# A state-space scan with a mixture of experts on one core: GpSimd makes two tiles of u by one instruction and adds dt's two parts

## The chip, the core and the metric

One core of a Trainium2 chip. The metric is the device time of one execution in microseconds (us). The text calls the engines TensorE (PE in rows), VectorE (DVE), ScalarE (ACT), GpSimd (POOL) and SyncE (SP, which only issues DMAs here; "SPq" in rows is its sequencer).

## What is computed

```python
xn = _layernorm(x)                      # x: 16 x 1024 x 256
dt = softplus(xn @ dt_w.T + dt_b)       # 256 features
A = -exp(log_A)                         # 256 x 32
b, c = xn @ B_w.T + B_b, xn @ C_w.T + C_b   # 32 states
h = exp(A * dt) * h + (dt * x) * b      # one step of time, 256 x 32 states
y = sum_n h * c + D_skip * x
out = x + y + moe(xn)                   # 8 experts, top 2, hidden 1024
```

softplus(v) is made as max(v, 0) + log(1 + exp(-|v|)): its first part and its logarithm are the "two parts" of dt.

## The kernel before, in words

After a preamble (layernorm, routing, the first dt values; it ends about 318 us into the execution) comes a loop over 128 **steps** on every engine. It is written as a loop over 8 experts whose body holds 16 steps written out, so every engine jumps back after each 16 steps.

The scan. A step covers 1024 time steps of one sequence and, of its 256 features and 32 states, 8 tiles `k` of 128 partitions (32 features x 4 states). Four steps (`ng` = 0 to 3) share one **half** of the features (`gh`), so a sequence is 8 steps and there are 32 halves in all. Of each tile:
- ScalarE makes the decay, `exp(a*dt)`, from tile `dt[k % 4]` into one of two PSUM buffers (`decay`, L798), two tiles ahead of the scan; `a_ready` counts them.
- GpSimd makes `u = dtx * b` into one of four SBUF buffers (L1027); `u_ready` counts them. A buffer comes free when the scan of four tiles before is done.
- VectorE scans (L1226) into `h`; `scan_done` counts. After tiles 0, 2, 4 and 6 it multiplies four tiles of `h` by `c` (`weigh`, L1215), and TensorE sums that over the states. The factor `c` is copied by ScalarE into PSUM bank 6 before each (`c_copy`, L868).

The prep. Each step also makes dt of 128 time steps for the next sequence: TensorE multiplies, ScalarE adds the bias into `zv` (L751), takes `|v|` and `exp` (L766, L768), and the logarithm into PSUM bank 6 (`log_part`, L772). At the end of the step VectorE forms `dt_n` from both by one instruction (`prep_dt`, L1131), and GpSimd multiplies it by x in the next step, after its tile 5 (`dtx_part`, L958). SyncE stores both in DRAM and the four tiles `dt` and the four tiles `dtx` are loaded from there when a new half begins: their loads are issued by SyncE during the **last step of a half** (`ng` = 3).

SyncE's order in that last step sets when these loads start. It works one list in order, each entry waiting for its own semaphores:

```python
next_b(0); next_dtx(0); store_dt; next_dtx(1); store_dtx; next_c(1)
next_dtx(2); next_dt(0); next_dtx(3); next_b(1)      # then w1, once in 16 steps
next_dt(1); next_dt(2); next_c(0); store_bc; next_dt(3)
```

(Written together here; in the code it is a list of calls with `if last:`.) `next_dtx(gp)` waits until u of tile 4 + gp of this step is made, `next_dt(gp)` until the decay of tile 4 + gp is.

The experts. Each step also pushes 256 slots through an expert: GpSimd gathers their rows by two indirect DMAs (L973) and scatters the result by two (L985); in two steps of eight it adds a block of y to the output by one more DMA (`add_y`, L990). TensorE works in program order: `moe_up(0), moe_up(1), quad(0), moe_up(2)`, the prep, `moe_up(3), quad(1)`, the transposes, `moe_down(0), quad(2), moe_down(1), quad(3)`; `quad(i)` sums the i-th weighing. ScalarE empties each product in between: `up_out` (L840) and `down_out` (L855), which stands behind the decay of the next step's tile 0 in ScalarE's own order; `c_copy(0)` stands behind the decay of the next step's tile 1, and `c_copy(2)` behind the emptying of the prep (`prep_out`), which waits for TensorE.

## Time and profile before

| what | value |
|---|---|
| median of 3 runs | 3790.76 us (3788.45 to 3792.91) |
| profiled execution, span | 3791.2 us |
| VectorE busy | 3645.0 us (96%) |
| GpSimd busy | 3268.7 us (86%) |
| TensorE busy | 3217.7 us (85%) |
| ScalarE busy | 2563.4 us (68%) |

The span of the profiled execution is taken as its time; it lies 0.4 us from the median. Busy shares are means over the preamble and the loop. "Idle before" in a row is idle time of the engine just before the instruction, and the arrow names what ended it.

### The profile page before, as it was taken

How to read it: one execution, taken by the hardware profiler on the slowest of the kernel's cores; microseconds unless marked ns; L12 is line 12 of the kernel's file. 1: busy time of each engine (PE TensorE's matmuls, PEld its weight loads, DVE VectorE, ACT ScalarE, POOL GpSimd, SP SyncE). 2: the span in 40 equal slices, each digit the busy share in tenths (PEclk: the TensorE clock that was granted, in tenths of full speed). 3: DMA queues.
4: the chain of work that ended last, by engine and by line, in shares of the span. 5: the costliest groups of instructions: out<-in, count | busy, mean ns of one | idle time of the engine just before them, and what ended most of it. 6: DMA issues, size and time to landing. Idle time of an engine off the chain costs nothing.

```text
span 3791.2 us, 64134 instructions
## 1 busy us (share of the span) xinstructions
PE 3217.7 (85%) x16548; PEld 2095.7 (55%) x16548; DVE 3645.0 (96%) x2281; ACT 2563.4 (68%) x4811; POOL 3268.7 (86%) x1722
## 2 busy tenths in 40 slices
PE   7776888888888888888888888888888888888887
PEld 4354555555555555555555555555555555555554
DVE  6787999999999999999999999999999999999998
ACT  3245677667776777767776777767776777677775
POOL 0017999999999999999999999999999999999996
PEclk9898999999999999999999999999999999999998
DMA  9974555555656556565656555465656555565666
GB/s 326 340 122 151 158 165 164 166 142 157 170 159 184 165 156 170 140 165 161 171 163 185 160 158 161 136 183 156 175 159 181 163 160 143 147 188 158 167 169 163
DMA packets 345249, 644.98 MB, mean 170 GB/s; under 512 B 49405, under 2 KB 221441, under 8 KB 344641
## 3 DMA queue, kind: packets, MB, share of 16 engines
q1 hardware_dynamic: 252018, 538.77, 44.1%
q0 software_dynamic: 67776, 85.24, 14.1%
q10 hardware_dynamic: 25104, 16.91, 2.0%
q8 instruction: 145, 2.38, 0.3%
q14 instruction: 206, 1.69, 0.1%
HBM read 515.55 MB, written 142.80 MB: 174 GB/s over the span
## 4 chain that ended last, share of the span: by engine, by line
DVE 36%; issue 28%; PE 9%; POOL 9%; ACT 8%; DMA 6%; DVEq 2%; SPq 1%; ACTq 0%; POOLq 0%
DVE hc L1215 18%; DVE h L1226 15%; POOL u L1027 5%; ACT bank L798 3%; DMA dt<-dt_rows 2%; PE bank L494 2%; PE bank L648 2%; PE bank L639 2%; POOL out_rows L985 2%; DMA dt<-x 2%; ACT xgt L802 1%; ACT za L766 1%; DVE dt_n L1131 1%; POOL xg L973 1%; ACT bank L868 1%
## 5 line engine op out<-in xcount | busy, mean ns | idle before, releaser
L1027 POOL TENSOR_TENSOR u<-dtx,b_sb 128x1024 f32<-128x1024 f32 x1024 | 2515.4, 2530 | 120.7 <-DVE h L1226 85.3
L1226 DVE TENSOR_TENSOR_SCAN h<-bank,u 128x1024 f32<-128x1024 f32 x1024 | 2301.8, 2279 | 17.4 <-POOL u L1027 11.5
L798 ACT ACTIVATE bank<-dt,a_neg 128x1024 f32<-128x1024 f32 x1026 | 1129.8, 1108 | 378.3 <-DVE h L1226 305.0
L639 PE MATMUL bank<-xgt,w_sb 128*128 128x256 f32 x4096 | 1027.9, 394 | 245.5 <-ACT ht L840 219.3
L1215 DVE TENSOR_TENSOR hc<-h,bank 128x2048 f32<-128x2048 f32 x514 | 1165.2, 2267 | 34.4 <-ACT bank L868 33.0
L639 PEld LDWEIGHTS bank<-xgt,w_sb 128*128 128x128 f32 x4096 | 745.6, 192 | 619.1 <-issue 536.2
L648 PE MATMUL bank<-w_sb,ht 128*128 128x256 f32 x4096 | 954.1, 387 | 26.0 <-ACT o_sb L855 24.6
L648 PEld LDWEIGHTS bank<-w_sb,ht 128*128 128x128 f32 x4096 | 774.4, 193 | 224.6 <-issue 125.3
L840 ACT ACTIVATE ht<-bank,b_sb 128x256 f32<-128x256 f32 x1024 | 423.6, 463 | 280.0 <-PE bank L639 279.9
L598 PE MATMUL bank<-hc,rsum 128*32 128x512 f32 x4112 | 549.3, 606 | 2.9 <-DVE hc L1215 2.9
L985 POOL DMA_INDIRECT out_rows<-o_sb,sidx x258 | 415.6, 1611 | 55.8 <-issue 34.5
L958 POOL TENSOR_TENSOR dtx_n<-dt_n,xnt 128x256 f32<-128x256 f32 x137 | 133.6, 975 | 272.3 <-DVE dt_n L1131 272.3
L973 POOL DMA_INDIRECT xg<-xn_rows,gidx x256 | 275.3, 1075 | 46.2 <-issue 44.2
L868 ACT ACTIVATE bank<-c_sb 128x512 f32<-128x512 f32 x512 | 303.1, 592 | 14.2 <-ACT bcv L756 2.8
L494 PE MATMUL bank<-ident,xg 128*128 128x128 f32 x516 | 87.2, 293 | 193.5 <-DVE hc L1215 178.6
L494 PEld LDWEIGHTS bank<-ident,xg 128*128 128x128 f32 x516 | 55.3, 143 | 310.0 <-DVE hc L1215 292.9
L598 PEld LDWEIGHTS bank<-hc,rsum 128*32 128x32 f32 x4112 | 80.9, 108 | 187.8 <-issue 184.1
L650 PE MATMUL bank<-b_row,ones 1*128 x512 | 177.7, 426 | 0.0
L855 ACT ACTIVATE o_sb<-bank,gate 128x256 f32<-128x256 f32 x256 | 119.4, 467 | 76.5 <-PE bank L650 70.3
L541 PE MATMUL bank<-xnt,dtw 128*128 128x128 f32 (+1 forms) x1104 | 151.1, 280 | 16.8 <-DVE hc L1215 14.2
L541 PEld LDWEIGHTS bank<-xnt,dtw 128*128 128x128 f32 x1104 | 137.2, 191 | 40.9 <-issue 35.5
L751 ACT ACTIVATE zv<-bank,dtb 128x128 f32<-128x128 f32 x276 | 86.5, 364 | 99.5 <-PE bank L548 98.1
(114 smaller groups left out, 1819.0 us busy)
## 6 DMA issues: line engine op xcount, KB each, us to landing
b_sb<-bc_rows SPq DMA_DIRECT2D x258, 512.0 KB
c_sb<-bc_rows SPq DMA_DIRECT2D x258, 512.0 KB, 4.0
dt<-dt_rows SPq DMA_DIRECT2D x132, 512.0 KB, 8.0
dtx<-dtx_rows SPq DMA_DIRECT2D x132, 512.0 KB, 5.2
w_sb<-w SPq DMA_DIRECT2D x18, 1024.0 KB
dt_rows<-dt_n SPq DMA_DIRECT2D x137, 128.0 KB
dtx_rows<-dtx_n SPq DMA_DIRECT2D x137, 128.0 KB
out_rows<-y_sb POOLq DMA_DIRECT2D x34, 512.0 KB
```

The lines of the kernel that those rows point to most:

```text
L541: mm = pe.matmul(z_ps[:, g * Q:(g + 1) * Q], dtw[:, k, g * P:(g + 1) * P], src, start=(k == 0), stop=(k == KD - 1))
L598: mm = pe.matmul(y_ps[c * RD:(c + 1) * RD, th, :], rsum[:], hc[:, GPP * th + c, :], start=False, stop=True, skip_group_check=True, tile_po ...
L639: mm = pe.matmul(m_ps[:, c, :], w1_sb[:, kk, ch * P:(ch + 1) * P], xgt[:, kk, :], start=(kk == 0), stop=(kk == KD - 1))
L648: pe.matmul(m_ps[:, j, :], ht[:, c, j * P:(j + 1) * P], w2_sb[:, c, :], start=(c == 0), stop=False)
L798: act.activation(a_ps[k % 2], dt[:, k % GPP, :], ACT.Exp, scale=a_neg[:, col:col + 1]).then_inc(a_ready, 1)
L840: ins = act.activation(ht[:, ch, :], m_ps[:, c, :], ACT.Relu, bias=b1_sb[:, bass.ds(e * HC + ch, 1)])
L868: act.activation(c_ps, c_sb[:, j, th * HALF:(th + 1) * HALF], ACT.Copy).then_inc(c_ready, 1)
L973: pool.indirect_dma_start(xg[:, buf, j, :], None, xn_d, rows, bounds_check=T - 1, oob_is_err=False).then_inc(xg_in, 16)
L985: pool.indirect_dma_start(outf, rows, o_sb[:, buf, j, :], None, bounds_check=T - 1, oob_is_err=False, compute_op=ALU.add).then_inc(o_scatt ...
L1027: pool.tensor_tensor(u[:, k % UB, :], dtx[:, gp, :], b_sb[:, j, :], ALU.mult).then_inc(u_ready, 1)
L1215: dve.tensor_tensor(hc[:, GPP * th:GPP * (th + 1), :], h[:, GPP * j:GPP * (j + 1), th * HALF:(th + 1) * HALF], c_ps.unsqueeze(1).to_broadc ...
L1226: dve.tensor_tensor_scan(h[:, k, :], a_ps[k % 2], u[:, k % UB, :], 0.0, ALU.mult, ALU.add).then_inc(scan_done, 1)
```

## The change

GpSimd makes tiles 2m and 2m+1 of u by one instruction of 2048 columns, with `b` broadcast over both, so a step has 4 of them where it had 8; `u_ready` counts pairs. A pair waits for the scans that free both its buffers, and at the start of a half for both tiles of `dtx`. Everything that waited for one tile of u waits for its pair. The instruction that forms `dt_n` leaves VectorE's loop; GpSimd does it in the next step, after its second pair, and `dtx_part` follows it there directly. [...] In the preamble VectorE still forms `dt_n`, but for the last one.

```diff
-        zv = sb("zv", [P, KD, Q])
+        zv = sb("zv", [P, 2, KD, Q])
+        zl = sb("zl", [P, 2, KD, Q])
...
+        NPR = NG // 2
...
                     def next_dtx(gp):
-                        sp.wait_ge(u_ready, st * NG + 4 + gp + 2)
+                        sp.wait_ge(u_ready, st * NPR + 2 + gp // 2 + 2)
...
                     def next_b(j):
-                        sp.wait_ge(u_ready, st * NG + 4 * j + 3 + 2)
+                        sp.wait_ge(u_ready, st * NPR + 2 * j + 1 + 2)
...
-            def softplus(p):
-                act.activation(za[:], zv[:], ACT.Abs).then_inc(za_done, 1)
+            def softplus(p, buf):
+                act.activation(za[:], zv[:, buf], ACT.Abs).then_inc(za_done, 1)
                 act.wait_ge(za_done, p + 1)
                 act.activation(ze[:], za[:], ACT.Exp, scale=-1.0).then_inc(ze_done, 1)
+                act.activation(zv[:, buf], zv[:, buf], ACT.Relu)
...
-                act.activation(zl_ps, ze[:], ACT.Ln, bias=1.0).then_inc(l_done, 1)
+                act.activation(zl[:, buf], ze[:], ACT.Ln, bias=1.0).then_inc(l_done, 1)
...
                         if i == 0:
                             act.wait_ge(c_in[1], 16 * (st + 2))
-                            act.wait_ge(dt_done, p + 2)
+                            act.wait_ge(hc_done, 4 * st + 5)
...
+            def dt_sum(p, buf):
+                pool.wait_ge(l_done, p + 1)
+                pool.wait_ge(dt_st, 16 * p + 1)
+                pool.wait_ge(prep_done, p + 1)
+                settle(pool)
+                pool.tensor_tensor(dt_n[:], zv[:, buf], zl[:, buf], ALU.add).then_inc(dt_done, 1)
...
-                    for k in range(NG):
-                        j, gp = k // GPP, k % GPP
+                    for m in range(NPR):
+                        j, gp = m // 2, 2 * (m % 2)
                         if gp == 0:
                             pool.wait_ge(b_in[j], 16 * (st + 1))
-                        if ng == 0 and k < GPP:
-                            pool.wait_ge(dtx_in[gp], 16 * (hf + 1))
-                        pool.wait_ge(scan_done, st * NG + k - UB + 1 + SCAN0)
-                        pool.tensor_tensor(u[:, k % UB, :], dtx[:, gp, :], b_sb[:, j, :], ALU.mult).then_inc(u_ready, 1)
+                        if ng == 0 and m < 2:
+                            for g in (gp, gp + 1):
+                                pool.wait_ge(dtx_in[g], 16 * (hf + 1))
+                        pool.wait_ge(scan_done, st * NG + 2 * m + 1 - UB + 1 + SCAN0)
+                        pool.tensor_tensor(u[:, gp:gp + 2, :], dtx[:, gp:gp + 2, :],
+                                           b_sb[:, j, :].unsqueeze(1).to_broadcast([P, 2, S]), ALU.mult).then_inc(u_ready, 1)
...
-                        if k == 5:
+                        if m == 1:
+                            dt_sum(NG + 1 + st, (s + 1) % 2)
                             dtx_part(NG + 1 + st, (b + 1 + (s + 1) // NG) % 2, (s + 1) % NG)
-                        if k in (4, 6):
-                            scatter(st, (s + 1) % 2, k // 2 - 2, 2 * b + ng if adds else None)
+                        if m >= 2:
+                            scatter(st, (s + 1) % 2, m - 2, 2 * b + ng if adds else None)
...
                 for k in range(NG):
-                    dve.wait_ge(u_ready, st * NG + k + 2)
+                    if k % 2 == 0:
+                        dve.wait_ge(u_ready, st * NPR + k // 2 + 2)
...
-                prep_dt(NG + 2 + st)
```

How GpSimd's order moves. In the middle of a step, before, from tile 4 on: u, a scatter, u of tile 5, the product `dtx_n`, and then (not shown) u of tile 6, a scatter, u of tile 7.

```order
L1027 TENSOR_TENSOR u<-dtx,b_sb 128x1024 [waits scan_done]
L980 ISA [waits sidx_done]
L985 DMA out_rows<-o_sb,sidx 16384x256 [waits evac_done]
L1026 REGISTER_ALU
L1027 TENSOR_TENSOR u<-dtx,b_sb 128x1024 [waits scan_done]
L955 REGISTER_ALU
L956 ISA [waits dt_done]
L958 TENSOR_TENSOR dtx_n<-dt_n,xnt 128x256 [waits dtx_st]
L1026 REGISTER_ALU
```

Now, from the second pair (tiles 2 and 3) on:

```order
L1039 TENSOR_TENSOR u<-dtx,b_sb 128x2048 [waits scan_done]
L984 DMA xg<-xn_rows,gidx 128x258
L959 ISA [waits l_done]
L962 TENSOR_TENSOR dt_n<-zv,zl 128x256 [waits dt_st,prep_done]
L966 REGISTER_ALU
L969 TENSOR_TENSOR dtx_n<-dt_n,xnt 128x256 [waits dt_done,dtx_st]
L1038 REGISTER_ALU [waits b_in1]
L1039 TENSOR_TENSOR u<-dtx,b_sb 128x2048 [waits scan_done]
L991 ISA [waits sidx_done]
L996 DMA out_rows<-o_sb,sidx 16384x256 [waits evac_done]
```

The sum and the product stand together between the second and the third pair, and the scatters behind the third and the fourth.

How SyncE's order stands in the last step of a half. It reads the same before and after (here: after), but its waits for `u_ready` are now for pairs: the first `dtx` row below needs the fourth pair, tiles 6 and 7, where it needed tile 6.

```order
L339 DMA dtx<-dtx_rows 128x1x1024 [waits u_ready,dtx_st]
L417 ISA
L339 DMA dt<-dt_rows 128x1x1024 [waits a_ready,dt_st]
L339 DMA dtx<-dtx_rows 128x1x1024 [waits u_ready,dtx_st]
L328 ISA [waits u_ready,b_st]
L328 ISA
L328 DMA b_sb<-bc_rows 128x1x1024
L417 REGISTER_ALU
L339 DMA dt<-dt_rows 128x1x1024 [waits a_ready,dt_st]
```

The rows are `next_dtx(2)`, `next_dt(0)`, `next_dtx(3)`, `next_b(1)`, `next_dt(1)`; nothing in them changed places.

## Rows read from the trace of the kernel before

**Rows 1.** The page's first line
```profile
span 3791.2 us, 64134 instructions
```

**Rows 2.** Groups of instructions: busy us, mean ns | idle before, its releasers
```profile
L1027 POOL TENSOR_TENSOR u<-dtx,b_sb 128x1024 f32<-128x1024 f32 x1024 | 2515.4, 2530 | 120.7 <-DVE h L1226 85.3 <-issue 21.7
L1226 DVE TENSOR_TENSOR_SCAN h<-bank,u 128x1024 f32<-128x1024 f32 x1024 | 2301.8, 2279 | 17.4 <-POOL u L1027 11.5 <-ACT bank L798 5.7
L798 ACT ACTIVATE bank<-dt,a_neg 128x1024 f32<-128x1024 f32 x1026 | 1129.8, 1108 | 378.3 <-DVE h L1226 305.0 <-DMA dt<-dt_rows 48.8 <-issue 17.3
```

**Rows 3.** Timeline of VectorE, one undisturbed step: start us, us, what, idle before
```profile
1940.97 0.40 DVE L1131 SCALAR_TENSOR_TENSOR dt_n<-zv,bank 128x256 f32<-128x256 f32 x1
1941.28 2.29 DVE L1226 TENSOR_TENSOR_SCAN h<-bank,u 128x1024 f32<-128x1024 f32 x1
...
1967.85 2.29 DVE L1226 TENSOR_TENSOR_SCAN h<-bank,u 128x1024 f32<-128x1024 f32 x1
```

**Rows 4.** Timeline of GpSimd around the start of a step with add_y
```profile
550.85 0.73 POOL L958 TENSOR_TENSOR dtx_n<-dt_n,xnt 128x256 f32<-128x256 f32 x1
551.54 2.37 POOL L1027 TENSOR_TENSOR u<-dtx,b_sb 128x1024 f32<-128x1024 f32 x1
554.06 1.60 POOL L985 DMA_INDIRECT out_rows<-o_sb,sidx  x1 [0.16 <-issue]
555.13 5.25 POOL L1027 TENSOR_TENSOR u<-dtx,b_sb 128x1024 f32<-128x1024 f32 x2
559.75 1.98 POOL L990 DMA_DIRECT2D out_rows<-y_sb  x1
562.03 1.11 POOL L973 DMA_INDIRECT xg<-xn_rows,gidx  x1 [0.30 <-issue]
...
566.81 7.01 POOL L1027 TENSOR_TENSOR u<-dtx,b_sb 128x1024 f32<-128x1024 f32 x3
```

**Rows 5.** Timelines at an undisturbed half's end: SyncE, ScalarE, VectorE
```profile
1927.80 0.54 SPq L338 DMA_DIRECT2D dt<-dt_rows  x1
...
1936.71 1.12 ACT L798 ACTIVATE bank<-dt,a_neg 128x1024 f32<-128x1024 f32 x1 [0.65 <-DVE h L1226]
...
1956.60 2.27 DVE L1215 TENSOR_TENSOR hc<-h,bank 128x2048 f32<-128x2048 f32 x1
```

**Rows 6.** Timelines at the loop's first half's end: SyncE
```profile
420.90 0.54 SPq L338 DMA_DIRECT2D dtx<-dtx_rows  x1
421.63 0.54 SPq L338 DMA_DIRECT2D dt<-dt_rows  x1
```

**Rows 7.** The same stretch, ScalarE
```profile
429.06 1.12 ACT L798 ACTIVATE bank<-dt,a_neg 128x1024 f32<-128x1024 f32 x1 [4.10 <-DMA dt<-dt_rows]
...
433.86 1.12 ACT L798 ACTIVATE bank<-dt,a_neg 128x1024 f32<-128x1024 f32 x1 [3.02 <-DMA dt<-dt_rows]
```

**Rows 8.** The same stretch, VectorE; it started this step at the first row
```profile
403.40 2.28 DVE L1226 TENSOR_TENSOR_SCAN h<-bank,u 128x1024 f32<-128x1024 f32 x1
...
431.62 2.29 DVE L1226 TENSOR_TENSOR_SCAN h<-bank,u 128x1024 f32<-128x1024 f32 x1
435.62 2.29 DVE L1215 TENSOR_TENSOR hc<-h,bank 128x2048 f32<-128x2048 f32 x1 [1.71 <-ACT bank L868]
...
450.49 2.29 DVE L1215 TENSOR_TENSOR hc<-h,bank 128x2048 f32<-128x2048 f32 x1 [1.65 <-ACT bank L868]
```

**Rows 9.** Timeline of TensorE, moe_down(1) in the same stretch and in another step
```profile
430.71 6.06 PE L648 MATMUL bank<-w_sb,ht 128*128 128x256 f32 x16 [3.65 <-ACT o_sb L855]
...
2019.42 3.72 PE L648 MATMUL bank<-w_sb,ht 128*128 128x256 f32 x16
```

**Rows 10.** Windows, columns: us, busy (x instructions) by engine, PEclk, DMA share, GB/s
```profile
431.00:434.00 3.00, 3.00 (x8) 2.37 (x8) 2.71 (x2) 0.14 (x1) 2.97 (x2) 0.50 1.03 400
```

**Rows 11.** Timeline of ScalarE across a jump back of the expert loop
```profile
2049.46 1.12 ACT L798 ACTIVATE bank<-dt,a_neg 128x1024 f32<-128x1024 f32 x1 [3.69 <-DMA dt<-dt_rows]
...
2055.52 1.12 ACT L798 ACTIVATE bank<-dt,a_neg 128x1024 f32<-128x1024 f32 x1 [3.94 <-issue]
```

More of the change, by code:

```diff
@@ L551, in prep @@
             def prep(p, par, q):
-                pe.wait_ge(dt_done, p + 1)
+                pe.wait_ge(bcv_done, p)
                 prep_z(par, q)
@@ L614, in _ @@
             pe.wait_ge(map_ready, 1)
-            pe.wait_ge(dt_done, NG + 3)
+            pe.wait_ge(bcv_done, NG + 2)
             pe.wait_ge(xg_in, 16 * SJ)
@@ L778, in low_part @@
                                scale=tokval[:, 0:1]).then_inc(low_ready, 1)
-            with act.Fori(0, NG) as q:
-                for o in range(OHQ):
-                    low_part(q * OHQ + o, o % 2)
-                    if o == 0:
-                        evac_prep(q)
-                        act.wait_ge(v_done, q + 1)
-                    if o == 1:
-                        softplus(q)
-                    if o == 2:
-                        log_part(q)
+            with act.Fori(0, NG // 2) as qq:
+                for i in range(2):
+                    q = qq * 2 + i
+                    for o in range(OHQ):
+                        low_part(q * OHQ + o, o % 2)
+                        if o == 0:
+                            evac_prep(q, i)
+                            act.wait_ge(v_done, q + 1)
+                        if o == 1:
+                            softplus(q, i)
+                        if o == 2:
+                            log_part(q, i)
             for p in (NG, NG + 1):
-                evac_prep(p)
+                evac_prep(p, p % 2)
                 act.wait_ge(v_done, p + 1)
-                softplus(p)
-                log_part(p)
+                softplus(p, p % 2)
+                log_part(p, p % 2)
             def decay(k, col):
@@ L925, in _ @@
                             act.wait_ge(v_done, p + 1)
-                            softplus(p)
+                            softplus(p, s % 2)
                             c_copy(3)
@@ L1019, in _ @@
                     adds = gh == 0 and ng in (1, 2)
-                    for k in range(NG):
-                        j, gp = k // GPP, k % GPP
+                    for m in range(NPR):
+                        j, gp = m // 2, 2 * (m % 2)
                         if gp == 0:
                             pool.wait_ge(b_in[j], 16 * (st + 1))
-                        if ng == 0 and k < GPP:
-                            pool.wait_ge(dtx_in[gp], 16 * (hf + 1))
-                        pool.wait_ge(scan_done, st * NG + k - UB + 1 + SCAN0)
-                        pool.tensor_tensor(u[:, k % UB, :], dtx[:, gp, :], b_sb[:, j, :], ALU.mult).then_inc(u_ready, 1)
-                        if k == 0 and adds:
+                        if ng == 0 and m < 2:
[4 more added lines that the diff above has]
+                                           b_sb[:, j, :].unsqueeze(1).to_broadcast([P, 2, S]), ALU.mult).then_inc(u_ready, 1)
+                        if m == 0 and adds:
                             pool.wait_ge(y_evac, 2 * hf + ng + 1)
@@ L1032, in _ @@
                             add_y((hf + 2 * B - 2 + ng - 1) % (2 * B), ng - 1)
-                        if k < SJ:
-                            gather(st + 1, (s + 1) % 2, k)
-                        if k == 5:
+                        if m < SJ:
+                            gather(st + 1, (s + 1) % 2, m)
+                        if m == 1:
+                            dt_sum(NG + 1 + st, (s + 1) % 2)
                             dtx_part(NG + 1 + st, (b + 1 + (s + 1) // NG) % 2, (s + 1) % NG)
-                        if k in (4, 6):
-                            scatter(st, (s + 1) % 2, k // 2 - 2, 2 * b + ng if adds else None)
+                        if m >= 2:
+                            scatter(st, (s + 1) % 2, m - 2, 2 * b + ng if adds else None)
             for j in range(SJ):
@@ L1130, in prep_dt @@
                 dve.wait_ge(prep_done, p + 1)
-                dve.scalar_tensor_tensor(out=dt_n[:], in0=zv[:], scalar=0.0, in1=zl_ps,
+                dve.scalar_tensor_tensor(out=dt_n[:], in0=zv[:, buf], scalar=0.0, in1=zl[:, buf],
                                          op0=ALU.max, op1=ALU.add).then_inc(dt_done, 1)
@@ L1180, in pairs @@
                 return t[:, bass.ds(g * OHB, OHB)].rearrange("p (i r) -> p i r", r=2).unsqueeze(2).to_broadcast([P, OHP, n, 2])
-            with dve.Fori(0, NG) as q:
-                for o in range(OHQ):
-                    g, buf = q * OHQ + o, o % 2
-                    dve.wait_ge(oh_used, g + 1)
-                    settle(dve)
-                    dve.tensor_tensor(oh_p[:, buf], wide(iota_pair, P), pairs(prt_h, g, P), ALU.is_equal).then_inc(ohp_done, 1)
-                    dve.tensor_tensor(oh_c[:, buf], wide(iota_pair, E * LPE), pairs(col_h, g, E * LPE), ALU.is_equal)
-                    dve.wait_ge(ohp_done, g + 1)
-                    dve.tensor_tensor(oh_high[:, buf], oh_p[:, buf], pairs(num_h, g, P), ALU.mult).then_inc(oh_ready, 1)
-                prep_dt(q)
-            prep_dt(NG)
-            prep_dt(NG + 1)
+            with dve.Fori(0, NG // 2) as qq:
+                for i in range(2):
+                    q = qq * 2 + i
+                    for o in range(OHQ):
+                        g, buf = q * OHQ + o, o % 2
+                        dve.wait_ge(oh_used, g + 1)
+                        settle(dve)
+                        dve.tensor_tensor(oh_p[:, buf], wide(iota_pair, P), pairs(prt_h, g, P), ALU.is_equal).then_inc(ohp_done, 1)
+                        dve.tensor_tensor(oh_c[:, buf], wide(iota_pair, E * LPE), pairs(col_h, g, E * LPE), ALU.is_equal)
+                        dve.wait_ge(ohp_done, g + 1)
+                        dve.tensor_tensor(oh_high[:, buf], oh_p[:, buf], pairs(num_h, g, P), ALU.mult).then_inc(oh_ready, 1)
+                    prep_dt(q, i)
+            prep_dt(NG, 0)
             dve.wait_ge(oh_used, 2 * NT // OHB + 2)
```

20 lines of the change are left out of this document (9 added, 11 removed).

## Prediction

> **What bounds the kernel now.** I read the page, then the groups, then timelines. The profiled execution spans 3791.2 us [rows 1], 0.4 us over the median of 3790.76, so the sum is made against 3791. The groups put the scans first on VectorE, with 17.4 us of idle time before 1024 of them; u on GpSimd, with 120.7 us, is the runner-up [rows 2]. The timeline of VectorE gives the pace: a step from its first scan to the next step's is 1967.85 - 1941.28 = 26.57 us, without a gap [rows 3]. Nearly all of the 128 steps have this length, so VectorE bounds the loop. What is off that pace is at the ends of halves, and there the transfers of the new half decide; that is where I put most of the working.
>
> **The removed instruction.** From the start of dt_n to the start of the scan behind it is 1941.28 - 1940.97 = 0.31 us [rows 3]; its own 0.40 overlaps its neighbour. A step of VectorE becomes 26.26 us, a pair of tiles with its weighing 6.565. That gives -0.31 x 128 = **-40 us**. Nothing hides it: VectorE is the bound.
>
> **GpSimd's new step.** A tile of u costs 7.01 / 3 = 2.34 us and dtx_n, 256 columns, 0.69 (550.85 to 551.54) [rows 4]. Between them lie 768 columns: 2.15 ns each and 0.14 fixed, so a pair of 2048 is 4.54. The bounds are 4.4 (columns alone) and 5.06 (twice the group's mean of 2.53 [rows 2], which counts overlapped time). A gather takes 1.11 and some 0.17 of issue, a scatter 1.07 + 0.16 and makes the next u later by 5.25 - 4.68 = 0.57, so 1.8; add_y adds 562.03 - 560.38 - 0.16 = 1.5 in two steps of eight [rows 4]. The sum of dt is like dtx_n, 0.69; the product now waits for it to be complete, for which I add 0.15 (estimate, by the gaps of 0.16 there). Together 4 x 4.54 + 2 x 1.28 + 2 x 1.8 + 2 x 0.69 + 0.15 = 25.85, where it was 8 x 2.34 + 2.56 + 3.6 + 0.69 = 25.57. GpSimd stays 0.4 us under VectorE's 26.26. For the add alone, 0.69 on GpSimd replaces 0.31 on VectorE. The Trainium skill (GPSIMD Engine Reference, Performance versus the Vector engine) would leave it where it was: its rule is that ordinary elementwise work stays on VectorE, since GpSimd is about half as fast. By the rule the move loses 0.38 us a step, by the trace it gains 0.31, since the engine that gets slower is not the bound.
>
> But the coupling is coarser. Pair m can start only when VectorE has begun pair m-1, and must be there 6.565 later: it may start late by 6.565 - 4.54 - 0.1 = 1.9 us. The lateness changes by 4.54 + what follows - 6.565: -0.7 after pair 0 (a gather), +0.8 after pair 1 (gather, sum, product), -0.2 after pairs 2 and 3. In an ordinary step it peaks at 0.9 and pair 3 starts 0.6 late: hidden. With add_y in two steps in a row it reaches 1.9 and VectorE waits about 1 us in eight steps: 16 x 1 = **+16 us** (bounds 0 and 25, by pairs of 4.4 and 4.7). The first pair of all is made while VectorE waits: **+2 us**. Relu on ScalarE stands between the exp and `c_copy(3)`. A decay of 1024 columns takes 1.12 [rows 7], so 256 take at most 0.5 (estimate). In an undisturbed step no weighing waits for a copy [rows 3], the scans of tiles 5 and 6 cover it, so I take nothing; without that cover it would be up to 0.5 x 128 = 64. The preamble keeps its instructions: 0.
>
> **The ends of halves.** SyncE issues the load of dt tile 0 behind that of dtx tile 2, which waited for u of tile 6. Before, it went out at 1927.80, 13.1 us after its step began (1941.28 - 26.57 = 1914.71), and the decay that needs it started at 1936.71, having waited for the scan alone [rows 3, 5]: in time. Now tile 6 comes with tile 7, whose buffer is free after the scan of tile 3: 2 x 6.565 = 13.1 us into the step. Add 0.6 of lateness and 4.54: 18.3; the loads go out one by one, 0.73 apart (420.90 to 421.63) [rows 6]: dt tile 0 at about 19.1, **6 us later** than before, the others behind it.
>
> The trace of before has one half's end just like that. In the loop's first steps GpSimd was still behind, and dt tile 0 was issued at 421.63, 18.2 us after the step's start at 403.40 [rows 6, 8]. The decay waited 4.10 us for it until 429.06, and the next decay 3.02 for tile 1 [rows 7]. The step after began at 431.62, where 403.40 + 26.57 = 429.97 was due; its first weighing waited 1.71 more [rows 8], as `c_copy(0)` stands behind the second decay. Then comes what costs most: `down_out(0)` stands behind the first decay, so TensorE waited 3.65 us for it, and took 6.06 us for sixteen products that take 3.72 elsewhere [rows 9], at a granted clock of 0.50, the lower level (1.2 GHz) [rows 10]. From there TensorE and ScalarE work without slack to `c_copy(2)`, and VectorE waited 1.65 for it until 450.49 [rows 8]. That is 450.49 - 403.40 = 47.1 us after the step's start; undisturbed it is 1956.60 - 1914.71 = 41.9 [rows 5]. This end cost **5.2 us**.
>
> There are 31 ends of halves inside the loop. In the new kernel each has this delay, 0.9 us worse (19.1 against 18.2), against a due time 0.31 earlier: 5.2 + 0.9 + 0.3 = 6.3 us, rounded down for what the two estimates are worth. At 23 of them nothing was lost before: 23 x 6.3 = **+145 us**. The first is the one above: +1. At 7 the expert loop jumps back and an expert's weights are loaded too; there the decays already waited 3.69 us for dt tile 1 and 3.94 for the jump [rows 11]. The dt tiles come some 5 us later there as well, but part of it falls beside the waits that exist; I take 4, **+28 us** (bounds 1 and 7). For the 23 the bounds are 3 (the two waits of VectorE at the step's start, 1.65 and 1.71, and TensorE's part absorbed) and 7.5 (a further 1.2 if the pairs are late by the 1.9 that they may be).
>
> **The sum:** 3791 - 40 + 16 + 2 + 145 + 1 + 28 = 3943; I say **3940 us**, 3.9% slower.
>
> **Rivals.**
> - *The loads still come in time (faster).* The load of dt tile 0 has from 19.1 to the end of scan 6, 22.0 us after the step's start (1936.71 - 1914.71), to land: 2.9 us. In favour: 7.4 us in rows 6 and 7 were measured among other transfers. Against: it would have to be less than half that. It decides at a landing time of about 3 us. Then -40 + 16 + 2 = -22: **3769 us**.
> - *Late, but cheap.* The two decays are late and TensorE's chain takes it up, as its wait is shorter or the clock stays up: 3 us at 23 ends, 1 at 7. 3791 - 40 + 18 + 69 + 7 = **3845 us**. Rows 8 speak against it: the third wait is as long as each of the others.
> - *GpSimd becomes the bound in every step.* A pair costs 5.06 and not 4.54: a step of GpSimd is 25.85 + 2.1 + 0.4 (add_y, mean) = 28.3, 1.8 over the old 26.57. 128 x 1.8 = 225, in which the ends' waits lie for the most part: about **4020 us**. For it: 0.4 us is thin. Against: one tile alone takes 2.37, and the mean of 2.53 holds what overlaps the tail of a scatter, 5.25 for two against 4.68 [rows 4].
> - *The change doesn't do what it says:* if the removed 0.31 came back as a wait (for the copy of c, which waited for dt_n and now for the weighing), only the -40 would go: 3983 us. Against: the copy has the 2.28 us of the next scan [rows 2, 3], and behind a decay of 1.12 [rows 7] needs some 0.6 of them (estimate: half the columns).
>
> **How the numbers follow.** Forecast 0.66; cheap delay 0.17; loads in time 0.06; GpSimd bound 0.09; the gain not there 0.02. A measurement of this kernel tells 0.2% (about 8 us) from no change. Only the second rival's lower edge comes near no change: its cost would have to be 1 us an end. I give 0.05 to that and 0.06 to faster, which leaves 0.89 for slower. The forecast's own bounds: 3791 - 40 + 69 + 7 + 2 = 3829 at the low end, 3791 - 40 + 25 + 2 + 173 + 2 + 49 = 4002 at the high one. They take in the cheap delay and the gain not there, and leave out the faster case and part of the third rival. Range **3825 to 4000**.
>
> **What would show it.** VectorE's undisturbed step at 26.26 us. The group of u at 4.5 us, x512, and little idle time before scans for u. At the ends of halves: SyncE issues dt tile 0 some 19 us into the step, ScalarE's decay waits 4 to 5 us for it, the decays' idle time put down to the load of dt grows from 48.8 us [rows 2] to 200 or more, and VectorE's weighings wait for the copy of c by over 100 us in all. TensorE's granted clock falls at each end. The prediction is wrong if the ends of halves keep the pace of their neighbours (then the landing time is what I misjudged), if ordinary steps are longer than 26.3 (then a pair costs more than 4.54), or if the load of dt is not behind that of dtx tile 2.

## The result and the profile after

The changed kernel takes **3952.11 us** (median of 4 runs, 3948.33 to 3960.42) against 3790.54 for the kernel before: a ratio of **1.0425, interval 1.0407 to 1.0443**. The forecast was 3940. The profiled execution spans 3946.5 us, 155.3 more than before [rows 1], and the working below is against that.

The first lines of the page of the changed kernel:

```profile
span 3946.5 us, 62062 instructions
...
PE 3281.4 (83%) x16548; PEld 2144.6 (54%) x16548; DVE 3617.5 (92%) x2152; ACT 2579.6 (65%) x4949; POOL 3291.3 (83%) x1338
```

VectorE is busy 27.5 us less than before (3645.0), and the span is 155 longer: the loss is idle time. The groups of instructions (busy us, mean ns | idle before, its releasers), which answer to [rows 2], say in front of what:

```profile
L1039 POOL TENSOR_TENSOR u<-dtx,b_sb 128x2048 f32<-128x2048 f32 x512 | 2411.0, 4709 | 241.1 <-DVE h L1242 194.4 <-DMA dtx<-dtx_rows 45.0 <-issue 0.3
L1242 DVE TENSOR_TENSOR_SCAN h<-bank,u 128x1024 f32<-128x1024 f32 x1024 | 2293.0, 2273 | 59.7 <-ACT bank L802 36.9 <-POOL u L1039 22.3
L1230 DVE TENSOR_TENSOR hc<-h,bank 128x2048 f32<-128x2048 f32 x514 | 1164.5, 2266 | 181.0 <-ACT bank L872 169.9 <-PE bank L599 10.0 <-ACT bank L943 0.7
L802 ACT ACTIVATE bank<-dt,a_neg 128x1024 f32<-128x1024 f32 x1026 | 1128.2, 1107 | 516.6 <-DVE h L1242 265.4 <-DMA dt<-dt_rows 230.2 <-issue 20.5
L649 PE MATMUL bank<-w_sb,ht 128*128 128x256 f32 x4096 | 1031.4, 409 | 147.7 <-ACT o_sb L859 147.7
```

GpSimd is not the bound: scans waited 22.3 us in all for u. The decays waited 230.2 us for the load of dt, where it was 48.8. The weighings waited 169.9 us for the copy of c, and TensorE's `moe_down` 147.7 us for an eviction of `o_sb`. The same two groups of the kernel before have 33.0 and 24.6 there:

```profile
L1215 DVE TENSOR_TENSOR hc<-h,bank 128x2048 f32<-128x2048 f32 x514 | 1165.2, 2267 | 34.4 <-ACT bank L868 33.0 <-ACT bank L940 0.7
...
L648 PE MATMUL bank<-w_sb,ht 128*128 128x256 f32 x4096 | 954.1, 387 | 26.0 <-ACT o_sb L855 24.6 <-issue 1.4
```

The timeline of VectorE over a quiet step and the end of a half (start us, us, what, idle before):

```profile
1840.64 2.26 DVE L1230 TENSOR_TENSOR hc<-h,bank 128x2048 f32<-128x2048 f32 x1
...
1866.88 2.26 DVE L1230 TENSOR_TENSOR hc<-h,bank 128x2048 f32<-128x2048 f32 x1
...
1888.74 2.28 DVE L1242 TENSOR_TENSOR_SCAN h<-bank,u 128x1024 f32<-128x1024 f32 x1
1892.14 2.29 DVE L1242 TENSOR_TENSOR_SCAN h<-bank,u 128x1024 f32<-128x1024 f32 x1 [1.12 <-ACT bank L802]
1896.47 2.29 DVE L1230 TENSOR_TENSOR hc<-h,bank 128x2048 f32<-128x2048 f32 x1 [2.03 <-ACT bank L872]
...
1911.62 2.29 DVE L1230 TENSOR_TENSOR hc<-h,bank 128x2048 f32<-128x2048 f32 x1 [1.92 <-ACT bank L872]
...
1938.47 2.29 DVE L1230 TENSOR_TENSOR hc<-h,bank 128x2048 f32<-128x2048 f32 x1 [0.47 <-ACT bank L872]
```

From the first weighing of one step to that of the next is 1866.88 - 1840.64 = **26.24 us**; before it was 26.57 [rows 3]. The last step of the half starts at 1864.68 (its first weighing less the 2.20 of a scan), and at its end the three waits that the prediction took from [rows 8] stand in a row: for the decay of tile 0, for `c_copy(0)`, for `c_copy(2)`. A fourth, 0.47, comes a step later, in front of the third weighing again; the prediction didn't have it.

SyncE's queue in that last step:

```profile
1883.36 0.55 SPq L339 DMA_DIRECT2D dtx<-dtx_rows  x1
1884.18 0.54 SPq L339 DMA_DIRECT2D dt<-dt_rows  x1
```

dt tile 0 goes out 1884.18 - 1864.68 = 19.5 us into the step; 13.1 before [rows 5]. (On the mean of the 23 ordinary ends it is 19.9 against 13.0.) ScalarE at the same end:

```profile
1890.91 1.12 ACT L802 ACTIVATE bank<-dt,a_neg 128x1024 f32<-128x1024 f32 x1 [4.57 <-DMA dt<-dt_rows]
1891.96 0.46 ACT L859 ACTIVATE o_sb<-bank,gate 128x256 f32<-128x256 f32 x1
...
1894.71 1.12 ACT L802 ACTIVATE bank<-dt,a_neg 128x1024 f32<-128x1024 f32 x1 [1.99 <-DMA dt<-dt_rows]
1895.77 0.58 ACT L872 ACTIVATE bank<-c_sb 128x512 f32<-128x512 f32 x1
...
1898.42 0.48 ACT L859 ACTIVATE o_sb<-bank,gate 128x256 f32<-128x256 f32 x1 [2.07 <-PE bank L651]
```

The two decays wait for dt tiles 0 and 1, and behind each stands what others wait for: `down_out(0)` behind the first, `c_copy(0)` behind the second. TensorE's side of it:

```profile
1892.56 5.11 PE L649 MATMUL bank<-w_sb,ht 128*128 128x256 f32 x16 [4.51 <-ACT o_sb L859]
```

and the window over these 16 products (us, busy by engine, PEclk, DMA share, GB/s):

```profile
1892.50:1897.50 5.00, 4.94 (x16) 4.00 (x16) 2.97 (x2) 1.86 (x3) 4.84 (x2) 0.71 0.94 377
```

After a wait of 4.51 us the granted clock is 0.71 on the mean of the five microseconds, between the two levels (0.50 is the 1.2 GHz one), and the products take 5.11 us where 3.72 is usual [rows 9, 10]. DMA is at 0.94: the load is not alone.

GpSimd in a quiet step, for the price of a pair and of the new sum:

```profile
2061.91 4.54 POOL L1039 TENSOR_TENSOR u<-dtx,b_sb 128x2048 f32<-128x2048 f32 x1 [0.78 <-DVE h L1242]
2066.61 1.06 POOL L984 DMA_INDIRECT xg<-xn_rows,gidx  x1 [0.16 <-issue]
2067.69 0.73 POOL L962 TENSOR_TENSOR dt_n<-zv,zl 128x256 f32<-128x256 f32 x1
2068.63 0.73 POOL L969 TENSOR_TENSOR dtx_n<-dt_n,xnt 128x256 f32<-128x256 f32 x1 [0.20 <-POOL dt_n L962]
2069.31 4.55 POOL L1039 TENSOR_TENSOR u<-dtx,b_sb 128x2048 f32<-128x2048 f32 x1
```

It still waits 0.78 us for VectorE: there is lead, as the 25.85 against 26.26 said.

For the whole loop I took the length of each of the 128 steps from the timeline of VectorE, before and after. "Excess" is what is over the quiet pace of the same kernel; an "ordinary" end is one inside the body of 16 steps, without the first.

| part | before, us | after, us | in the sum |
|---|---|---|---|
| quiet step | 26.57 | 26.24 | -0.33 x 128 = -42 |
| excess of an ordinary half's end (23) | 0.0 | 6.1 | +140 |
| excess of an end at the loop's jump (7) | 4.96 | 9.3 | +30 |
| the first end | 5.2 | 6.6 | +1 |
| the third step of each sequence, its second with `add_y` (16) | 0.04 | 0.7 | +11 |
| the step behind an end (31) | 0.1 | 0.6 | +17 |
| first scan of the loop, start | 321.97 | 316.65 | -5 |
| behind the loop | | | +4 |

These make 156 of the 155.3.

### The profile page after: what moved, and what is told of

Its sections match the earlier page's. It is cut to its first block, busy times and chain, and to the rows that moved or that the text cites. A ratio compares the mean times of both kernels' runs of the same rounds, so it can differ in the third digit from the quotient of the medians.

```text
span 3946.5 us, 62062 instructions
## 1 busy us (share of the span) xinstructions
PE 3281.4 (83%) x16548; PEld 2144.6 (54%) x16548; DVE 3617.5 (92%) x2152; ACT 2579.6 (65%) x4949; POOL 3291.3 (83%) x1338
## 4 chain that ended last, share of the span: by engine, by line
issue 43%; POOL 23%; PE 13%; DMA 12%; ACT 4%; DVE 2%; SPq 1%; POOLq 1%; ACTq 0%; DVEq 0%
POOL u L1039 13%; PE bank L649 6%; DMA out_rows<-o_sb,sidx 5%; POOL xg L984 4%; POOL out_rows L996 4%; PE bank L640 3%; DMA dtx<-dtx_rows 2%; DMA dt<-x 2%; POOL dt_n L962 2%; PE bank L599 1%; DMA dtx_rows<-dtx_n 1%; DMA dt<-dt_rows 1%; ACT ht L844 1%; ACT bank L802 1%; PE bank L651 1%
## 5 line engine op out<-in xcount | busy, mean ns | idle before, releaser
L1039 POOL TENSOR_TENSOR u<-dtx,b_sb 128x2048 f32<-128x2048 f32 x512 | 2411.0, 4709 | 241.1 <-DVE h L1242 194.4
L1242 DVE TENSOR_TENSOR_SCAN h<-bank,u 128x1024 f32<-128x1024 f32 x1024 | 2293.0, 2273 | 59.7 <-ACT bank L802 36.9
L1230 DVE TENSOR_TENSOR hc<-h,bank 128x2048 f32<-128x2048 f32 x514 | 1164.5, 2266 | 181.0 <-ACT bank L872 169.9
L640 PE MATMUL bank<-xgt,w_sb 128*128 128x256 f32 x4096 | 1020.1, 392 | 242.9 <-ACT ht L844 221.4
L649 PE MATMUL bank<-w_sb,ht 128*128 128x256 f32 x4096 | 1031.4, 409 | 147.7 <-ACT o_sb L859 147.7
L640 PEld LDWEIGHTS bank<-xgt,w_sb 128*128 128x128 f32 x4096 | 740.2, 190 | 613.9 <-issue 532.9
L649 PEld LDWEIGHTS bank<-w_sb,ht 128*128 128x128 f32 x4096 | 828.0, 207 | 369.4 <-issue 246.8
L969 POOL TENSOR_TENSOR dtx_n<-dt_n,xnt 128x256 f32<-128x256 f32 x137 | 125.1, 913 | 287.7 <-DVE dt_n L1145 241.3
```

The lines of the kernel that those rows point to most:

```text
L640: mm = pe.matmul(m_ps[:, c, :], w1_sb[:, kk, ch * P:(ch + 1) * P], xgt[:, kk, :], start=(kk == 0), stop=(kk == KD - 1))
L649: pe.matmul(m_ps[:, j, :], ht[:, c, j * P:(j + 1) * P], w2_sb[:, c, :], start=(c == 0), stop=False)
L1039: pool.tensor_tensor(u[:, gp:gp + 2, :], dtx[:, gp:gp + 2, :], b_sb[:, j, :].unsqueeze(1).to_broadcast([P, 2, S]), ALU.mult).then_inc(u_re ...
L1230: dve.tensor_tensor(hc[:, GPP * th:GPP * (th + 1), :], h[:, GPP * j:GPP * (j + 1), th * HALF:(th + 1) * HALF], c_ps.unsqueeze(1).to_broadc ...
L1242: dve.tensor_tensor_scan(h[:, k, :], a_ps[k % 2], u[:, k % UB, :], 0.0, ALU.mult, ALU.add).then_inc(scan_done, 1)
```

## The experiments

The theory: at each half's end the load of dt tile 0 is issued 6 us later, because it stands behind a load that waits for a pair; what that delays costs 6 us at 23 ends and 4 more than before at 7. Rivals: the pairs themselves or the sum on GpSimd cost the time in ordinary steps; Relu on ScalarE does; the ends are dear because of the amount that is moved there, in whatever order; or it is not the load as such but the order of ScalarE behind it.

**The loads of dt ahead of those of dtx tiles 2 and 3** (`e1_dt_first`), the rest as changed:

```diff
                     if last:
-                        next_dtx(2)
                         next_dt(0)
+                        next_dt(1)
+                        next_dt(2)
+                        next_dtx(2)
                         next_dtx(3)
...
-                    if last:
-                        next_dt(1)
-                        next_dt(2)
```

> The changed kernel, but SyncE issues the loads of dt tiles 0, 1 and 2 ahead of those of dtx tiles 2 and 3. Theory A (the late load of dt behind the pair of u makes the ends of halves dear): dt tile 0 goes out 3 us earlier, about 16.6 us into the step, the two waits at the step's start shrink to under 1.5 us together, but dtx tiles 2 and 3 land later and the second pair costs about 1.3; an end costs 1.5 to 2.5 where it cost 6.1: about 3835 us, between 3800 and 3870. Theory B (the ends are dear because of the amount moved there at once, whatever the order): stays at 3950 within 15 us.

Measured: 3850.81 us, ratio 1.0157 (1.0140 to 1.0174). 101 of the 162 us are gone by reordering five issues. An ordinary end costs 2.5 us in place of 6.1. But dtx tiles 2 and 3 are late now, and the groups show the new wait in front of the scans:

```profile
L1241 DVE TENSOR_TENSOR_SCAN h<-bank,u 128x1024 f32<-128x1024 f32 x1024 | 2297.3, 2276 | 119.4 <-POOL u L1038 85.7 <-ACT bank L801 32.2
```

It was 22.3 us for u in the changed kernel.

**The same delay put into the kernel before** (`e3_before_late`): neither pairs nor the moved sum, only a wait of SyncE.

```diff
                         next_dtx(2)
+                        sp.wait_ge(scan_done, st * NG + 5 + 1 + SCAN0)
+                        settle(sp)
                         next_dt(0)
```

> The kernel before, with one thing more: in the last step of a half SyncE waits for the scan of tile 5 before it loads dt tile 0, so that this load goes out about 20 us into the step where it went out at 13.1. Nothing of GpSimd, VectorE or ScalarE is changed. Theory A: an end costs about 6 us as in the changed kernel, 23 x 6 + 7 x 4 + 1: about 3960 us, between 3930 and 3985. Theory B' (the pairs of u or the sum on GpSimd cost it): stays at 3791 within 15 us.

Measured: 3909.09 us, ratio 1.0308 (1.0291 to 1.0326): a late issue alone costs 118 us, so the mechanism is the right one, but the size is 51 us under what I expected, and 21 under the lower bound. SyncE and then ScalarE, in a last step that starts at 1849.30:

```profile
1869.32 0.53 SPq L338 DMA_DIRECT2D dt<-dt_rows  x1
...
1873.90 1.12 ACT L800 ACTIVATE bank<-dt,a_neg 128x1024 f32<-128x1024 f32 x1 [3.19 <-DMA dt<-dt_rows]
...
1879.03 1.12 ACT L800 ACTIVATE bank<-dt,a_neg 128x1024 f32<-128x1024 f32 x1 [3.34 <-DMA dt<-dt_rows]
```

The issue is at 20.0, as late as in the changed kernel, but the decay starts at 1873.90 - 1849.30 = 24.6 and not at 26.2. Here dtx tile 2 went out long before (7.7 us); in the changed kernel it goes out 0.82 us ahead of dt tile 0. The trace has the landings too: from issue to landing dt tile 0 takes 4.1 us here and 6.3 in the changed kernel (medians of the 23 ordinary ends). An end costs 3.3 us, and the third wait, for `c_copy(2)`, is 0.4 us on the mean against 1.8. The load's place in the row is a second part of the delay, next to the time of its issue.

**Each half of the change alone.** `e4_single_u` is the changed kernel with u tile by tile, `e5_pairs_only` the kernel before with the pairs (and VectorE's sum as it was).

```diff
-                        pool.wait_ge(scan_done, st * NG + 2 * m + 1 - UB + 1 + SCAN0)
-                        pool.tensor_tensor(u[:, gp:gp + 2, :], dtx[:, gp:gp + 2, :],
-                                           b_sb[:, j, :].unsqueeze(1).to_broadcast([P, 2, S]), ALU.mult).then_inc(u_ready, 1)
+                        pool.wait_ge(scan_done, st * NG + k - UB + 1 + SCAN0)
+                        pool.tensor_tensor(u[:, k % UB, :], dtx[:, gp, :], b_sb[:, j, :], ALU.mult).then_inc(u_ready, 1)
```

> The changed kernel with u made tile by tile again (8 instructions a step, buffers freed one by one); the sum of dt stays on GpSimd, after tile 5. GpSimd's step is 8 x 2.34 + 2.56 + 3.6 + 1.38 + 0.2 = 26.4 us against VectorE's 26.24, so it loses its lead slowly, above all in the two steps with add_y. Theory A: the load of dt tile 0 goes out at about 14 us in one half of a sequence and at 17 in the other, so every second end costs about 2: 3791 - 42 + 32 - 5 = 3776, between 3750 and 3805. If the sum on GpSimd (and not the pairs) were what makes the changed kernel slow: over 3900.

Measured: 3828.53 us, ratio 1.0104 (1.0087 to 1.0121), 53 over the expectation and outside its range. Quiet steps are 26.24 as planned. But GpSimd now does all the old work and the sum besides. In the halves with `add_y`, which use up its lead, dt tile 0 goes out 15.4 us into the last step in the first sequence of an expert and 17.7 in the second, and an end costs 2.0 and 3.7 us; in the other halves inside an expert it goes out at 14.6 and an end costs 0.6. The sum on GpSimd is not free by itself: its 0.7 us come out of the lead that the loads live on.

> The kernel before with u made in pairs, and nothing else: dt_n stays on VectorE. Theory A: steps of 26.57, ends of halves as dear as in the changed kernel: 3791 + 23 x 6 + 7 x 4 + 1 = 3958, between 3935 and 3980. If the sum on GpSimd were the cause: within 15 us of 3791.

Measured: 3938.35 us, ratio 1.0396 (1.0377 to 1.0416), 148 over the kernel before, of 162 in all. Quiet steps are 26.57, an end costs 4.9, and the decay of dt tile 0 starts 25.5 us into the step. So the pairs make most of the loss, and not by their price: the group of u has a mean of 4709 ns for two tiles in the changed kernel, less than twice the 2530 of [rows 2].

**dt tile 0 loaded ahead of dtx tile 0, dt tile 1 ahead of dtx tile 2** (`e6_dt_before_dtx`):

```diff
                     if last:
+                        next_dt(0)
                         next_dtx(0)
...
                     if last:
+                        next_dt(1)
                         next_dtx(2)
-                        next_dt(0)
                         next_dtx(3)
...
                     if last:
-                        next_dt(1)
                         next_dt(2)
```

> The changed kernel, with SyncE loading dt tile 0 ahead of dtx tile 0 in the last step of a half (about 11 us into the step, where its decay is made), tile 1 ahead of dtx tile 2, tile 2 behind b. Theory A: dt tiles 0 and 1 land before they are wanted, the waits of the decays for them nearly vanish, and with them TensorE's wait and fall of the clock; dtx tiles 2 and 3 land a little late. An end costs 0 to 2 us where it cost 6.1, the waits of 0.6 in the step after an end go as well: 3952 - 23 x 5 - 7 x 3 - 12 = 3804, between 3780 and 3835. Theory B (the amount moved): above 3850, as the first reordering left it.

Measured: **3781.62 us** (10 runs), ratio **0.9975 (0.9966 to 0.9985)**: all of the loss is gone and the kernel is 8.5 us faster than the one before. SyncE and ScalarE at the end whose last step starts at 1795.8:

```profile
1806.14 0.56 SPq L339 DMA_DIRECT2D dt<-dt_rows  x1
...
1817.81 1.12 ACT L802 ACTIVATE bank<-dt,a_neg 128x1024 f32<-128x1024 f32 x1 [0.34 <-DVE h L1242]
...
1822.19 1.12 ACT L802 ACTIVATE bank<-dt,a_neg 128x1024 f32<-128x1024 f32 x1 [2.56 <-DVE h L1242]
```

Issued at 10.3; the decays wait for the scans again, as in [rows 5]. The groups of the weighings and of `moe_down`:

```profile
L1230 DVE TENSOR_TENSOR hc<-h,bank 128x2048 f32<-128x2048 f32 x514 | 1162.3, 2261 | 28.2 <-ACT bank L872 27.0 <-ACT bank L943 0.7
...
L649 PE MATMUL bank<-w_sb,ht 128*128 128x256 f32 x4096 | 955.2, 387 | 21.2 <-ACT o_sb L859 21.2
```

An ordinary end costs 0.4 us. The pairs, the sum on GpSimd, Relu and the amount moved are the changed kernel's; only SyncE's order differs. No run puts this order into the kernel before, so how the 8.5 us are shared between the change and the new order is not shown.

**The order of ScalarE, with the loads late as they are.** `e7_down_first` takes `down_out(0)` ahead of the decay of tile 0 in last steps; `e8_down_and_copy` also `c_copy(0)` ahead of that of tile 1; `e10_act_three` also `down_out(1)`. The last of them:

```diff
+                        if tng == 0 and k == 6:
+                            down_out(0)
+                        if tng == 0 and k == 7:
+                            c_copy(0)
+                            down_out(1)
                         if tng == 0 and tk < GPP:
                             act.wait_ge(dt_in[tk], 16 * (2 * b + ts // HPB + 1))
...
                         if k == 6:
-                            down_out(0)
+                            if tng != 0:
+                                down_out(0)
...
                         if k == 7:
-                            c_copy(0)
-                            down_out(1)
+                            if tng != 0:
+                                c_copy(0)
+                            if tng != 0:
+                                down_out(1)
```

> The changed kernel, its loads untouched; in the last step of a half ScalarE empties the product of moe_down(0) before the decay of the next half's tile 0, not behind it. Theory A says that the third wait of an end (1.9 us before weighing 2, and 0.5 in the step after) comes only through TensorE, which waits for that emptying and is at the low clock afterwards. Then this wait goes and the first two (1.2 before the scan, 2.2 before the first weighing) stay: an end costs 3.7: 3952 - 23 x 2.4 - 7 x 1.5 - 15 = 3871, between 3850 and 3895. If the third wait had its cause in the late loads of dt tiles 2 and 3 or of c instead, nothing changes (3952 within 10).

Measured: 3946.93 us, ratio 1.0408 (1.0385 to 1.0430): 5 us gained where 81 were expected, and even those 5 are within the spread of the runs (3936.35 to 3954.19, the changed kernel's 3948.33 to 3960.42). TensorE at such an end, and a window over its last row (columns as above):

```profile
1892.04 3.72 PE L649 MATMUL bank<-w_sb,ht 128*128 128x256 f32 x16
...
1901.42 3.75 PE L640 MATMUL bank<-xgt,w_sb 128*128 128x256 f32 x8 [4.04 <-ACT o_sb L859]
...
1901.40:1905.20 3.80, 3.75 (x8) 2.51 (x8) 3.80 (x2) 0.98 (x1) 2.42 (x3) 0.50 0.62 194
```

`moe_down(1)` takes its usual 3.72 without a wait. The wait has gone one place on, to `moe_up(0)`, which needs the bank that `down_out(1)` empties, and that one stands behind the second decay. Its eight products take 3.75 us where they take 1.99 undisturbed, at a granted clock of 0.50. In the groups 147.7 us of wait at L649 have become 13.7, and 130.5 new ones stand at L640:

```profile
L640 PE MATMUL bank<-xgt,w_sb 128*128 128x256 f32 x4096 | 1098.2, 415 | 355.6 <-ACT ht L844 219.6 <-ACT o_sb L859 130.5 <-ACT xgt L806 4.4
```

So this run moved TensorE's wait and its low clock; it didn't take them away.

> As the run with the emptying first, and the copy of c for the first weighing also stands ahead of the decay of tile 1. Theory A: the wait of 2.2 before the first weighing goes too; what is left is the scan that waits 1.2 for the decay of tile 0, and at most 0.5 before the scan of tile 1: an end costs 1.2 to 2, 23 x 4.4 + 7 x 4 + 15 less than the changed kernel: 3808, between 3785 and 3835, with the loads as late as ever.

Measured: 3928.46 us, ratio 1.0368 (1.0346 to 1.0391), also a miss, by 120 us. The weighings' wait for the copy halves (169.9 to 84.9), and the scans' wait for decays grows from 36.9 to 112.1:

```profile
L1248 DVE TENSOR_TENSOR_SCAN h<-bank,u 128x1024 f32<-128x1024 f32 x1024 | 2293.8, 2274 | 135.5 <-ACT bank L802 112.1 <-POOL u L1045 23.2
L1236 DVE TENSOR_TENSOR hc<-h,bank 128x2048 f32<-128x2048 f32 x514 | 1163.6, 2264 | 89.3 <-ACT bank L872 84.9 <-ACT bank L949 4.3
```

The decays themselves start when they did (26.4 and 30.6 us into the last step at an ordinary end, 26.3 and 30.3 in the changed kernel). VectorE, no longer held at the weighing, comes to the scans earlier and waits there. TensorE still waits 120.8 us at L640 for `down_out(1)`.

> The changed kernel with its loads as late as ever; in the last step of a half ScalarE empties both products of moe_down and makes the copy of c ahead of the decays for which it waits. The runs before left TensorE waiting one place further on (4.0 us behind the second emptying, which stood behind the decay of tile 1). If that chain is the cause of the third wait, it goes now: an end costs the 1.2 before the scan, up to 0.5 before the next and little else: 3952 - 23 x 4 - 7 x 3 - 15 = 3824, between 3795 and 3850. If the third wait comes from the late tiles 2 and 3 of dt or from c, it stays and the time is near 3928.

Measured: 3876.74 us, ratio 1.0222 (1.0206 to 1.0238), 53 over the expectation and outside its range. ScalarE at the end whose last step starts at 1832.9:

```profile
1855.35 0.48 ACT L859 ACTIVATE o_sb<-bank,gate 128x256 f32<-128x256 f32 x1 [0.84 <-PE bank L651]
1858.71 1.12 ACT L802 ACTIVATE bank<-dt,a_neg 128x1024 f32<-128x1024 f32 x1 [2.88 <-DMA dt<-dt_rows]
...
1860.07 0.58 ACT L872 ACTIVATE bank<-c_sb 128x512 f32<-128x512 f32 x1
1860.62 0.47 ACT L859 ACTIVATE o_sb<-bank,gate 128x256 f32<-128x256 f32 x1
1862.56 1.12 ACT L802 ACTIVATE bank<-dt,a_neg 128x1024 f32<-128x1024 f32 x1 [1.46 <-DMA dt<-dt_rows]
```

The decay of tile 0 starts at 25.8 (26.4 on the mean), as late as ever, and an ordinary end costs 2.5 us instead of 6.1. So some 3.6 of the 6.1 is what three small instructions of ScalarE make of the late loads by standing behind the decays, TensorE's wait and low clock included: TensorE's waits for an eviction of `o_sb` are down to 13.4 us at L649 and 5.5 at L640. Of the 2.5 left, 1.1 is VectorE's wait for the late decay of tile 0 and 0.9 still its wait for `c_copy(2)`. The third instruction, `down_out(1)`, brings 52 of the 75 us, with the other two already moved; it alone was not tried. What lies over the expectation is in the 2.5 left at each ordinary end (23 x 2.5 = 57 us in all) and at the loop's jumps, where a step became longer rather than shorter (31.6 us for 30.9, 10 us over 14 steps).

**The two cures together**, to see what is left: `e9_all_pairs` (e6 and e8), `e11_pairs_best` (e6 and e10), `e12_single_best` (the same with single tiles of u).

> Both: the loads of dt early and ScalarE's two instructions ahead of its decays, with pairs of u. An end costs 0 to 1 us; left are the two steps with add_y (0.7 in eight steps: 12 us) and the jumps of the loop (about 4 each, as before the change). 3791 - 42 - 5 + 12 + 10 = 3766, between 3750 and 3790, so faster than the kernel before.

> Pairs of u, early loads of dt, and ScalarE's three instructions ahead of its decays. The ends already cost next to nothing with the early loads; what is left are add_y's two steps (1.5 us in eight) and the jumps of the loop (4.5 each), where the second emptying could save 1 to 2: 3775, between 3765 and 3785.

> The same with u tile by tile. GpSimd's step is 26.4 us and 27.9 with add_y, 214.4 in eight steps against VectorE's 209.9, so GpSimd bounds the kernel on the mean, though it never stops VectorE for its pairs: 16 x 214.4 + 340 = 3770, between 3760 and 3785. If it is well above the version with pairs, the pairs are worth having once the loads are early.

Measured: 3784.08 (0.9984, 0.9974 to 0.9994), 3784.77 (0.9975, 0.9963 to 0.9987), 3786.06 (0.9983, 0.9975 to 0.9992). The first two came out at or near the upper edge of what was expected, the third 1 us above its range. With the loads in time ScalarE's order has nothing left to mend, and pairs or single tiles make no difference that these runs can tell. e6 is as fast as any of them with the fewest edits.

**Relu done twice** (`e13_relu_twice`), with a wait between. (In the changed kernel ScalarE applies Relu to `zv` in place, one more instruction of 256 columns a step; it takes 0.40 us.)

```diff
+                act.activation(zv[:, buf], zv[:, buf], ACT.Relu).then_inc(relu_done, 1)
+                act.wait_ge(relu_done, p + 1)
                 act.activation(zv[:, buf], zv[:, buf], ACT.Relu)
```

> The changed kernel with the Relu done twice (with a wait between, so some 0.45 us more on ScalarE in each step, ahead of the copy of c for weighing 3). If the Relu is covered, as the prediction says, 3952 within 8 us; if it lies on the path, up to 0.45 x 128 = 58 more.

Measured: 3955.25 us, ratio 1.0429 (1.0414 to 1.0444), against 1.0425: no difference. A Relu here is covered.

The ends, on the mean of the 23 ordinary ones. The decay of tile 0 is counted from the last step's start; the third wait is VectorE's for `c_copy(2)`; the low clock is the time at a granted clock of 0.50 in the stretch from 22 to 50 us after the last step's start.

| kernel | decay of tile 0, us | third wait, us | low clock, us | an end costs, us |
|---|---|---|---|---|
| before | 22.0 | 0 | 0 | 0.0 |
| e6 | 22.2 | 0.1 | 0 | 0.4 |
| e3 | 24.3 | 0.4 | 3.0 | 3.3 |
| e5 | 25.5 | 1.9 | 5.3 | 4.9 |
| changed | 26.3 | 1.8 | 5.6 | 6.1 |
| e7 (same loads, ScalarE's order changed) | 26.4 | 1.3 | 7.1 | 5.7 |
| e8 (the same) | 26.4 | 1.6 | 5.9 | 4.9 |
| e10 (the same) | 26.4 | 0.9 | 2.5 | 2.5 |

## Why the prediction was right, point by point

- **The removed instruction**, -0.31 a step by the gap between starts: measured -0.33, -42 us for -40. Taking the gap and not the duration of 0.40 was right.
- **A pair at 4.54**, the sum like `dtx_n`, 0.15 for the dependence: 4.54, 0.73 and 0.20. The group's mean of 4709 ns is again above one that runs alone; whoever had taken it would have seen GpSimd as the bound. The third rival falls.
- **`add_y` +16:** about +11. The rule of the Trainium skill (GPSIMD Engine Reference, Performance versus the Vector engine) that elementwise work stays on VectorE would have put 0.38 us more on each step; quiet steps got 0.33 shorter, so by the pace it doesn't hold here. But `e4_single_u` shows a price that neither the rule nor the comparison of steps tells of: the sum alone made the kernel 1% slower, since GpSimd's lead was in use elsewhere.
- **Relu for nothing:** so shown by `e13_relu_twice`.
- **The fourth rival**, the removed 0.31 coming back as a wait for the copy of c, falls by the quiet step of 26.24 without a gap.
- **dt tile 0 at about 19.1, 6 us later:** 19.5, and 6.4 later, at the end shown; 19.9, and 6.9 later, on the mean. The first rival needed a landing time under 2.9 us. The decay started 6.7 us after the issue here, and 4.6 in `e3_before_late` where nothing of SyncE's stood close ahead.
- **6.3 us an end:** 6.1 at the 23 ordinary ends, and +30 for +28 at the loop's jumps. The one end in the trace of before that already had the delay was a good model. The second rival, late but cheap, took 3 us an end and falls; an end did cost 3.3 in `e3_before_late`, where the load landed some 2 us sooner.
- **What was wrong in it: "then comes what costs most"**, said of TensorE's wait for `down_out(0)`, its low clock and the third wait behind them. At the 23 ordinary ends the third wait is 1.8 us; the wait for `c_copy(0)` before the first weighing is 2.2, and the one for the decay 0.9. And `down_out(0)` was too narrow a name for what holds TensorE: `e7_down_first` freed it, and TensorE waited for `down_out(1)` instead, as long and with more low clock behind it. Only `e10_act_three` rid TensorE of the wait, and there the third wait and the low clock halve. TensorE's part was there as predicted, then, but it hangs on two emptyings behind two decays. What the low clock costs by itself no run shows.
- **Missing:** the 0.6 us in the step behind each end (+17), nearly all of it a wait of 0.5 for the copy of c before the third weighing. [rows 8] ended with the third weighing, and I had not read on.
- **The start, +2:** it was 5.3 us earlier instead (316.65, before 321.97). The first pair does cost its time, but the preamble got shorter. The change makes TensorE's preparation there wait for `bcv_done` in place of `dt_done`, so it no longer waits for the sum. All eleven kernels with that edit start the loop at 314.55 to 318.57, and `e3_before_late` and `e5_pairs_only` without it at 319.88 and 322.35. That fits, but other edits came with it, and it alone was not tried.

The total came out well in part by cancelling. Over the sum of 3943 lie 17 (the step behind an end), 4 (behind the loop) and 2 (the jumps), under it 7 at the start, 5 at the ordinary ends, 5 for `add_y` and 2 for the removed instruction.

Open: why the ends at the loop's jump keep some 2.7 us a step over the pace in the best versions too (28.95 in e6, two steps each). And of the 42 us that quiet steps gain, e6 keeps 8.5: the two steps with `add_y` take 26.95 and 27.28 us there, 0.9 more than before where 0.66 less was due, which is 16 x 1.55 = 25 us. Single tiles bring the second of them to 26.35 (`e12_single_best`), but the first step behind the ends in mid-sequence takes 27.33 there, where it takes 26.41 in e6, and its loop is 6.5 us longer than that of e6.

## What to carry to other kernels

An instruction made twice as large is paid for where something waits for its first half: here a transfer whose issue waited for tile 6 and now waited for tile 7 too, in a queue where other loads stood behind it. Before merging, list every wait on the merged count, and in each in-order queue put the issue that is needed first ahead of the one that waits longest. Here two loads moved forward in SyncE's order made the changed kernel 170 us faster. And when a late arrival costs more than its lateness, look at what stands behind the waiting instruction on its own engine, all of it together: of the 162 us lost, freeing the first of three gave back 5 (within the spread of the runs), two of them 24, and all three 75.
